# Two transformer blocks on one core: q and k as two-part fp32r rows in 32-row strips

## The chip, the cores and the metric

One core of a Trainium2 chip runs the whole program. The metric is the device time of one launch in microseconds, lower is better.

## The reference

Two conditioned transformer blocks run one after the other on x of shape (2, 512, 144): two sequences (b) of 512 tokens, width C = 144, 16 heads of 9. Both blocks have this form:

```
mod = silu(c) @ W_ada + b_ada                 # shift, scale, gate, twice
h = layernorm(x) * (1 + scale) + shift
q, k, v = h @ W_qkv + b_qkv
a = softmax(q k^T / 3) v                      # per head; block 1: causal mask
x = x + gate * (a @ W_proj + b_proj)
h = layernorm(x) * (1 + scale2) + shift2
x = x + gate2 * (act(h @ W_fc1 + b1) @ W_fc2 + b2)   # act: gelu in block 0, silu in block 1
```

The hidden width of the MLP is 576. Everything is float32. The program calls block 0 "layer 0" and block 1 "layer 1".

## The kernel before

Each of the five engines runs a list written at build time. `steps()` gives every piece of work (an item) a duration and what it has to follow; `plan()` puts the items of each engine in order and gives every TensorE item one of seven PSUM banks. There are streams: "max" (row maxima of the scores), "shift" (the maxima brought into the stacks), "attend" (scores and exps), "gather" (probs times V), and "side" (heads, tails, MLPs). The engines take their lists strictly in order, with semaphore waits inside.

Attention goes by groups of four heads, 16 groups in all: 8 in layer 0 and 8 in layer 1. For each group, TensorE first forms the scores with queries on partitions (L1129, 16 products of up to 512 keys), VectorE takes the negated row maximum of each (L1014), GpSimd splits the maxima in three bf16 parts (L768 to L771), TensorE transposes them (L1137), ScalarE copies them (L831) and a DMA of GpSimd puts them in rows of the q stack (L778). Then TensorE forms the scores once more with keys on partitions (L1147); with the extra rows they come out less their maximum, and ScalarE takes the exp (L841). The pv product (L1167) writes the four heads of a group in four column strips of one bank, with a column of ones for the sum. In layer 1 both score products have only the columns that the causal mask leaves (128, 256, 384 or 512), and a 128x128 matmul with the identity adds the mask to the diagonal block (L1131, L1150).

The scores have float32 accuracy through parts: q and k are each split in three bf16 parts, and six products of parts are stacked, 6 x 9 rows and three for the maximum, in tiles of 96 rows, QS and KS. To make them, the projection writes d-major rows, ScalarE and VectorE form the parts (L820, L995 to L998), SP writes them to DRAM (`qk_parts`, L638, L646) and reads them back into the stacks with repetition (L668). The stacks have to be zero first (L738 to L740, L823). In layer 1 the restack of a sequence follows its last layer-0 score product.

A wide projection (q/k and fc1, `wide_product`, L1064 to L1067) takes four fp32r matmuls: main channels high x high, high x low, low x high, and the 16 last channels with the bias in a stacked operand. VectorE forms the parts of the activations (L977 to L983) and ScalarE with GpSimd or VectorE those of the weights (`wsplit`). The gate products (L1095, L1096) and V (L1116) use plain fp32, which the trace shows as two records per matmul.

Of the kernel before, what the change touches and what calls it, by code (L numbers as in the profile page):

```python
# [7 lines left out]
U32 = mybir.dt.uint32  # L29
# [4 lines left out]
P = 128  # L34
# [9 lines left out]
QK = 2 * C  # L44
QKW = [128, 128, QK - 256]
# [4 lines left out]
SR = 96  # L50
EPS = 1e-6
# [7 lines left out]
Q_RUNS = [(0, 1, 3), (1, 1, 2), (2, 1, 1)]  # L59
K_RUNS = [(0, 3, 1), (0, 2, 1), (0, 1, 1)]  # L60
PRODUCTS = 6
MROW = PRODUCTS * D
KROWS = 96


# [13 lines left out]
def head_items(l, b):  # L79

    return ([("stats", l, b, 0, 0), ("norm", l, b, 0, 0), ("hT", l, b, 0, 1, 0), ("hT", l, b, 0, 0, 0)]
            + [("qk", l, b, c) for c in (2, 0, 1)] + [("v", l, b, i) for i in range(2)])


def mlp_items(l, b, s):

    items = []
    for c in range(NF + 2):
        if c < NF:
            items.append(("fc1", l, b, c, s))  # L90
        if c >= 1 and c - 1 < NF:
            items.append(("tanh", l, b, c - 1, s))
        if c >= 2:
            items.append(("gate", l, b, c - 2, s))
    return items


def tail_items(l, b):

    if part_with(l, b, 0) == 0:  # L100
        return ([("aT", l, b, r, 0) for r in range(2)] + [("proj", l, b, i) for i in range(2)]
                + [("stats", l, b, 1, 0), ("norm", l, b, 1, 0), ("hT", l, b, 1, 1, 0), ("hT", l, b, 1, 0, 0)]
                + mlp_items(l, b, 0) + [("fc2", l, b, i) for i in range(2)])
    items = [("aT", l, b, r, s) for s in (1, 2) for r in range(2)]
    items += [("proj", l, b, 0), ("stats", l, b, 1, 1), ("proj", l, b, 1), ("norm", l, b, 1, 1), ("stats", l, b, 1, 2),
              ("hT", l, b, 1, 1, 1), ("hT", l, b, 1, 0, 1), ("norm", l, b, 1, 2), ("hT", l, b, 1, 1, 2), ("hT", l, b, 1, 0, 2)]
# [3 lines left out]

SIDE = ([("stats", 0, 0, 0, 0), ("acol", 0, 0), ("norm", 0, 0, 0, 0), ("wsplit", 0, 0)] + head_items(0, 0)[2:4]
        + head_items(0, 1)[:1] + head_items(0, 0)[4:] + head_items(0, 1)[1:]
# [3 lines left out]
WEIGHTS = ([("acol", 0, 1), ("wsplit", 0, 1), ("wsplit", 1, 0), ("wsplit", 1, 1), ("acol", 1, 0), ("acol", 1, 1)]  # L116
           + [("agate", l, b) for l in range(L) for b in range(B)])
GROUPS = L * B * NG
BANKS = 7

# [11 lines left out]
def steps():  # L132

    out = []

    def add(stream, engine, item, ns, *after):
        out.append((stream, engine, item, ns, after))

    cost = {"acol": (950, 350), "agate": (980, 370), "v": (660, 370), "proj": (980, 370), "fc2": (2460, 370)}

    loaded = {("acol", 0, 0): 5500, ("wsplit", 0, 0): 7500, ("wsplit", 0, 1): 15500, ("stats", 0, 0, 0, 0): 4500,
              ("stats", 0, 1, 0, 0): 9500,
              ("acol", 0, 1): 36000, ("agate", 0, 0): 60000}
    norm = None
    for item in SIDE + WEIGHTS:
        kind, l, *rest = item
        b = rest[0]
        size = 0.5 if kind in ("stats", "norm", "hT", "aT", "fc1", "tanh", "gate") and rest[-1] else 1  # L150
        stream = "side" if item in SIDE else "weights"
        if kind in cost:
            after = {"acol": [], "agate": [],
                     "v": [("DVE", ("hT", l, b, 0, 0, 0))],
                     "proj": [*(("ACT", ("aT", l, b, r, part_with(l, b, rest[-1]))) for r in range(2)), ("POOL", ("agate", l, b))],
                     "fc2": [("DVE", ("gate", l, b, NF - 1, part_with(l, b, rest[-1])))]}[kind]
            add(stream, "PE", item, cost[kind][0], *after, loaded.get(item, 0))
            add(stream, "DVE", item, cost[kind][1], ("PE", item))
            if kind == "agate":
                add(stream, "POOL", item, 3200, ("DVE", item), 66000)  # L160
            if kind == "fc2" and l == L - 1:
                add("side", "SP", item, 500, ("DVE", item))
        elif kind == "wsplit":
            add(stream, "ACT", item, 1700, loaded.get(item, 0))
            if stream == "side":
                add(stream, "DVE", item, 1100, ("ACT", item))
            else:
                add(stream, "POOL", item, 6500 if b else 3500, ("ACT", item), 19000)
        elif kind == "stats":
# [4 lines left out]
            add("side", "POOL", item, 960, ("DVE", item), 0 if l or k or not b else 18500)  # L174
        elif kind == "norm":
            after = [("POOL", ("stats", *item[1:]))]
            if norm and norm != item[:4]:
                after += [("PE", ("hT", *norm[1:], r, 0)) for r in range(2)]
            norm = item[:4]
            add("side", "DVE", item, 1060 * size, *after)  # L180
        elif kind == "hT":
            k, r, _ = rest[1:]
            add("side", "PE", item, 430 * size, ("DVE", ("norm", l, b, k, rest[-1])))
            add("side", "ACT", item, (600 * size + 60), ("PE", item), ("DVE", ("acol", l, k)))

            add("side", "DVE", item, (1400 if r else 1070) * size + 2100 * (item[1:] == (0, 0, 0, 0, 0)), ("ACT", item))
        elif kind == "qk":
            add("side", "PE", item, 860, ("DVE", ("hT", l, b, 0, 0, 0)), ("POOL", ("wsplit", l, 0)) if l else ("DVE", ("wsplit", 0, 0)))
            c = rest[1]
            add("side", "ACT", item, 4000 if (l, b, c) == (0, 0, 1) else 480, ("PE", item))  # L190
            add("side", "DVE", item, 1700, ("ACT", item))
            after = [("PE", ("scores", (b + 1) * NG - 1, 15))] if l and c < 2 else []
# [1038 lines left out]
```

## Time and profile before

| | us |
|---|---|
| median of 3 runs | 380.48 |
| fastest, slowest | 379.99, 384.52 |
| span of the profiled execution, which is its time in the profile | 382.2 |

A row of the timeline has start, duration, engine, line, operation and the tiles, output first; x4 is a run of four. "96*128 96x512" is a weight tile of 96 rows and 128 columns and a moving tile of 96 rows and 512 columns. TensorE's ends are modelled and overlap, so distances between starts are what tells the pace. PE is TensorE, PEld its weight loads, DVE VectorE, ACT ScalarE, POOL GpSimd, SP SyncE. PEclk is the granted clock of TensorE, 1 at 2.4 GHz. fp32r tiles are named f32 in matmul rows.

### The profile page before, as it was taken

What the parts mean: (1) busy time and instruction counts of PE and PEld (TensorE: products, weight loads), DVE (VectorE), ACT (ScalarE), POOL (GpSimd) and SP (SyncE); (2) the same over time, 40 slices, a digit from 0 to 9 for tenths busy, and PEclk for the clock granted to TensorE, in tenths of its full rate; (3) what the DMA queues carried; (4) which work ended last, traced back from release to release, by engine and by line L of the source; (5) the groups of instructions that cost most, each with busy time, mean ns of one, the idle gap of its engine ahead of it and who ended that gap; (6) DMA issues with size and microseconds to landing.
All of it is one profiled execution on the core that took longest, in us unless ns stands there. A gap on an engine that the chain in (4) does not pass through costs nothing.

```text
span 382.2 us, 5927 instructions
## 1 busy us (share of the span) xinstructions
PE 305.8 (80%) x2020; PEld 165.7 (43%) x2020; DVE 260.8 (68%) x575; ACT 195.1 (51%) x414; POOL 72.8 (19%) x157
## 2 busy tenths in 40 slices
PE   2044399697999999889993879999953999999567
PEld 2023282122334363445341545565431565647366
DVE  6999589674858798996851667879633668831363
ACT  4037310274573755894781127745613456894352
POOL 5934500010102615501100010110100011010000
PEclk9999585588989999999997968999968799999969
DMA  6402645420000000000044100000451000000000
GB/s 173 116 0 79 143 92 157 103 72 17 1 2 2 0 4 1 2 1 3 1 121 100 60 7 0 3 1 13 128 96 53 3 1 3 3 1 17 16 2 31
DMA packets 11285, 15.57 MB, mean 41 GB/s; under 512 B 1774, under 2 KB 9909, under 8 KB 10824
## 3 DMA queue, kind: packets, MB, share of 16 engines
q1 hardware_dynamic: 10744, 15.00, 14.9%
q8 instruction: 16, 0.26, 0.3%
q0 software_dynamic: 512, 0.20, 0.2%
q14 instruction: 13, 0.11, 0.1%
HBM read 10.67 MB, written 4.13 MB: 39 GB/s over the span
## 4 chain that ended last, share of the span: by engine, by line
PE 53%; DVE 17%; DMA 14%; issue 6%; ACT 5%; SPq 4%; POOL 1%; DVEq 0%; ACTq 0%; POOLq 0%
PE PB L1147 11%; PE OB L1167 10%; DMA KS<-qk_parts 10%; PE PB L1129 9%; PE PB L1209 5%; DVE hn L968 4%; DMA QS<-mT 3%; SPq L668 3%; DVE negm L1014 3%; PE PB L1104 3%; DVE parts L998 2%; DVE rest L995 2%; PE PB L1174 2%; PE PB L1064 2%; PE PB L1150 1%
## 5 line engine op out<-in xcount | busy, mean ns | idle before, releaser
L1014 DVE TENSOR_REDUCE negm<-PB 128x1 f32<-128x512 f32 (+3 forms) x256 | 136.3, 583 | 62.4 <-PE PB L1131 39.2
L841 ACT ACTIVATE probs<-PB 128x512 f32<-128x512 f32 (+3 forms) x256 | 116.4, 521 | 80.2 <-PE PB L1150 47.0
L1129 PE MATMUL PB<-KS,QS 96*128 96x512 bf16 (+3 forms) x256 | 87.2, 387 | 21.1 <-DMA KS<-qk_parts 20.3
L1147 PE MATMUL PB<-QS,KS 96*128 96x512 bf16 (+3 forms) x256 | 81.4, 360 | 8.5 <-DMA QS<-mT 6.9
L1167 PE MATMUL OB<-probs,V 128*10 128x512 f32 (+3 forms) x512 | 59.7, 538 | 0.9 <-ACT probs L841 0.6
L1129 PEld LDWEIGHTS PB<-KS,QS 96*128 96x128 bf16 x256 | 26.2, 105 | 65.5 <-issue 42.0
L1147 PEld LDWEIGHTS PB<-QS,KS 96*128 96x128 bf16 x256 | 25.0, 101 | 52.9 <-issue 34.1
L768 POOL CAST msp<-negm 128x16 bf16<-128x16 f32 x16 | 4.3, 266 | 161.6 <-DVE negm L1014 161.6
L1104 PE MATMUL PB<-ident,hn 128*16 128x128 f32 (+1 forms) x64 | 12.1, 336 | 22.7 <-DVE hn L968 22.7
L1131 PE MATMUL PB<-mask_qk,identb 128*128 128x128 bf16 x128 | 29.4, 244 | 0.0
L1150 PE MATMUL PB<-mask_kq,identb 128*128 128x128 bf16 x128 | 27.0, 226 | 0.0
L831 ACT ACTIVATE mT<-PB 12x512 bf16<-12x512 bf16 x16 | 9.3, 581 | 27.2 <-PE PB L1137 27.1
L1036 DVE TENSOR_TENSOR X<-X,PB 128x288 f32<-128x288 f32 x16 | 7.3, 453 | 21.4 <-PE PB L1209 16.7
L1209 PE MATMUL PB<-g_fc,U 128*128 128x144 f32 (+1 forms) x160 | 20.7, 287 | 0.0
L735 POOL TENSOR_TENSOR rstd<-veps,half 128x4 f32<-128x4 f32 (+1 forms) x9 | 8.7, 969 | 61.8 <-DVE veps L958 61.7
L1209 PEld LDWEIGHTS PB<-g_fc,U 128*128 128x128 f32 (+1 forms) x160 | 20.0, 190 | 0.7 <-issue 0.4
L968 DVE TENSOR_SCALAR hn<-X,mean,rstd 128x144 f32<-128x144 f32 x32 | 19.5, 685 | 1.0 <-POOL rstd L735 1.0
L1053 DVE SCALAR_TENSOR_TENSOR U<-U,xh 128x512 f32<-128x512 f32 (+3 forms) x25 | 14.2, 578 | 8.0 <-ACT xh L877 7.5
L810 ACT ACTIVATE hT_r<-PB,mod_r 16x512 f32<-16x512 f32 (+1 forms) x9 | 6.5, 724 | 25.7 <-PE PB L1104 25.4
L1104 PEld LDWEIGHTS PB<-ident,hn 128*16 128x16 f32 (+1 forms) x64 | 7.7, 140 | 27.1 <-issue 13.4
L778 POOL DMA_DIRECT2D QS<-mT x16 | 9.6, 598 | 48.3 <-ACT mT L831 48.3
L850 ACT ACTIVATE OT<-OB 128x512 f32<-128x512 f32 x16 | 9.6, 599 | 16.2 <-PE OB L1167 16.2
(135 smaller groups left out, 453.6 us busy)
## 6 DMA issues: line engine op xcount, KB each, us to landing
qk_parts<-parts SPq DMA_DIRECT2D x8, 384.0 KB, 2.5
QS<-qk_parts SPq DMA_DIRECT2D x4, 324.0 KB
KS<-qk_parts SPq DMA_DIRECT2D x4, 324.0 KB
QS<-qk_parts SPq DMA_DIRECT2D x8, 108.0 KB
KS<-qk_parts SPq DMA_DIRECT2D x8, 108.0 KB
QS<-qk_parts SPq DMA_DIRECT2D x4, 216.0 KB
KS<-qk_parts SPq DMA_DIRECT2D x4, 216.0 KB
X<-in_x SPq DMA_DIRECT2D x2, 288.0 KB, 3.2
```

What stands on the lines that cost most here:

```text
L668: sp.dma_start(dst[row0:row0 + rows, h0:h1, :], src).then_inc(stacked[l * B + b][i], 16)
L841: nc.scalar.activation(probs[:, kt % 2, j, q0:T], bank_of(item)[:, q0:T], ACT.Exp, scale=SCALE).then_inc(bank_free[BANK[item]], 1)
L968: ins = nc.vector.tensor_scalar(hn[:, t, :], X[b][:, t, :], mean[:, t, 0:1], rstd[:, t:t + 1], ALU.subtract, ALU.mult)
L1014: nc.vector.tensor_reduce(negm[:, g % 2, qt, j:j + 1], bank[:, 0:keys_of(g // (B * NG), qt)], AX.X, ALU.max, negate=True).then_inc(bank_fr ...
L1053: nc.vector.scalar_tensor_tensor(u, u, 1.0, xh[0:w, c, tokens(s)], ALU.add, ALU.mult).then_inc(g_ready, 1)
L1104: ins = nc.tensor.transpose(bank[0:n, t * P:(t + 1) * P], src, ident[:, :])
L1129: ins = nc.tensor.matmul(o[:, 0:w], q, KS[b][0:KROWS, h + j, 0:w], start=True, stop=(l == 0))
L1131: ins = nc.tensor.matmul(o[:, w - P:w], identb[:, :], mask_qk[:, :], start=False, stop=True)
L1147: ins = nc.tensor.matmul(bank[:, q0:T], KS[b][0:KROWS, h + j, kt * P:(kt + 1) * P], QS[b][0:KROWS, h + j, q0:T], start=True, stop=(l == 0))
L1150: ins = nc.tensor.matmul(bank[:, q0:q0 + P], identb[:, :], mask_kq[:, :], start=False, stop=True)
L1167: ins = nc.tensor.matmul(OB[CT * j:CT * j + VW, q0:T], V[b][:, kt, h + j, :], probs[:, kt % 2, j, q0:T], start=(kt == 0), stop=(kt == NT - 1))
L1209: ins = nc.tensor.matmul(bank[:, t * C:(t + 1) * C], U[0:w, c, tok], g_fc2[l][b][0:w, c, :], start=(c == 0), stop=(c == NF - 1))
```

## The change

q and k now stay in SBUF. One head takes a strip of 32 partitions: 9 rows high, 9 rows high or low, 9 rows low or high, two rows for the maximum (high and low part) and three of zeros; four heads of a group fill 128 partitions. The projection's weights have the columns of a head three times, the low one negated, so one product writes all rows of a group; ScalarE rounds it to fp32r in the tile `QK`, and one VectorE pass subtracts, which leaves the low part where `low_row` is 1. The main channels are plain fp32, the last 16 channels with the bias one stacked fp32r operand. This stack is now made before the transpose ("hr" on VectorE, with modulation by rows). The maxima reach the q rows by matmul with an fp32r identity. The scores are products of 32 rows; the order of units goes through the heads first (`UNITS`). fc1 is also fp32 and one stack, layer 1's gate reads PSUM. The weights of layer 0 are spread by ScalarE, VectorE and GpSimd at the start, those of layer 1 by GpSimd ("stackw", "fcs"). The DMA through DRAM, the clearing of the stacks and the DMA of the maxima are gone. ScalarE's queue loads the first x and W_qkv. The durations in `steps()` were changed too.

```diff
-            + [("qk", l, b, c) for c in (2, 0, 1)] + [("v", l, b, i) for i in range(2)])
+            + [("qk", l, b, 0, w) for w in range(2)] + [("v", l, b, i) for i in range(2)]
+            + [("qk", l, b, g, w) for g in range(1, NG) for w in range(2)])
...
+UNITS = [(t, j) for t in range(NT) for j in range(HG)]
...
+        def strip(j):
+            return slice(CT * j, CT * j + CT)
+        def spread(w, which):
+            v = heads_in(w, which)
+            return (v[:, :, 0:3:2, :] if which else v[:, :, 0:2, :]), v[:, :, LOW[which]:LOW[which] + 1, :]
...
 (SP)
-                    sp.dma_start(scratch[l, b, c, :, 0:D - 1].rearrange("s d h t -> (d h) s t"),
-                                 parts[:, c, :, :]).then_inc(parts_out[c], 16)
...
-                                sp.dma_start(dst[row0:row0 + rows, h0:h1, :], src).then_inc(stacked[l * B + b][i], 16)
...
 (GpSimd)
-                        nc.gpsimd.memset(KS[0][0:KROWS, :, :].bitcast(U32), 0).then_inc(k_zeroed[0], 1)
...
+                    spread_heads(w_qk_s[0], w_s[0], 0).then_inc(wide_stack, 1)
+                    fill_late()
...
+                    link(nc.gpsimd.tensor_copy(s[:, :, :, MROW], m))
+                    nc.gpsimd.tensor_tensor(s[:, :, :, MROW + 1], m, s[:, :, :, MROW].bitcast(F32),
                                             ALU.subtract).then_inc(msplit_ready, 1)
-                    pool.dma_start(QS[b][MROW:MROW + 3, h:h + HG, :], mT[:, g % 2, :]).then_inc(m_in[g % 2], 16)
...
 (ScalarE)
+            act.dma_start(X[0][:, :, :], a["x"][0].rearrange("(t p) c -> p t c", p=P)).then_inc(x_in[0], 16)
...
+                    nc.scalar.activation(QK[b][:, g, w, :], bank_of(item), ACT.Copy).then_inc(high_ready, 1)
...
+                    nc.scalar.activation(QM[:, g % 2, :], bank_of(item), ACT.Copy).then_inc(bank_free[BANK[item]], 1)
...
 (VectorE)
+                    link(nc.vector.tensor_tensor(y, hn[:, t0:t1, P:C], row_of(SC), ALU.mult))
+                    link(nc.vector.tensor_tensor(y, y, row_of(SH), ALU.add))
...
+                    nc.vector.tensor_copy(hs[:, t0:t1, 65:65 + R], y)
+                    link(nc.vector.tensor_copy(hs[:, t0:t1, 1:1 + R], y))
+                    nc.vector.tensor_tensor(hs[:, t0:t1, 33:33 + R], y, hs[:, t0:t1, 1:1 + R].bitcast(F32),
+                                            ALU.subtract).then_inc(hr_ready, 1)
...
+                    s = QK[b][:, g, w, :]
+                    ins = nc.vector.scalar_tensor_tensor(s, bank, low_row[:, w:w + 1], s.bitcast(F32), ALU.mult, ALU.subtract)
...
 (TensorE)
+                    nc.tensor.matmul(bank, w_qk[l][:, w, cols], hT[:, :], start=True, stop=False)
+                    nc.tensor.matmul(bank, w_qk_s[l][:, w, cols], hT_s[:, :], start=False, stop=True).then_inc(filled_bank, 1)
...
-                    ins = nc.tensor.matmul(o[:, 0:w], q, KS[b][0:KROWS, h + j, 0:w], start=True, stop=(l == 0))
+                    rows = strip(j)
+                    ins = nc.tensor.matmul(bank[:, 0:w], QK[b][rows, g % NG, 0, qt * P:(qt + 1) * P],
+                                           QK[b][rows, g % NG, 1, 0:w], start=True, stop=(l == 0))
                     if l:
-                        ins = nc.tensor.matmul(o[:, w - P:w], identb[:, :], mask_qk[:, :], start=False, stop=True)
+                        ins = nc.tensor.matmul(bank[:, w - P:w], identb[:, :], mask_qk[:, :], start=False, stop=True)
...
+                    nc.tensor.matmul(bank, identr[:, :], QK[b][:, g % NG, 0, :], start=True, stop=False)
                     for t in range(NT):
-                        ins = nc.tensor.transpose(bank.bitcast(BF16)[0:3 * HG, t * P:(t + 1) * P],
-                                                  msp[:, t, :, :].rearrange("p s j -> p (s j)"), identb[:, :])
+                        ins = nc.tensor.matmul(bank[:, t * P:(t + 1) * P], msp[:, t, :], identr[:, :], start=False, stop=(t == NT - 1))
...
-                    ins = nc.tensor.matmul(bank[:, q0:T], KS[b][0:KROWS, h + j, kt * P:(kt + 1) * P],
-                                           QS[b][0:KROWS, h + j, q0:T], start=True, stop=(l == 0))
+                    ins = nc.tensor.matmul(bank[:, q0:T], QK[b][rows, g % NG, 1, kt * P:(kt + 1) * P],
+                                           QM[rows, g % 2, q0:T], start=True, stop=(l == 0))
                     if l:
                         ins = nc.tensor.matmul(bank[:, q0:q0 + P], identb[:, :], mask_kq[:, :], start=False, stop=True)
...
-                        ins = nc.tensor.matmul(o, aT_r[:, tok], g_proj_r[l][b][:, :], start=False, stop=True)
+                        ins = nc.tensor.matmul(o, aT_r[0:R + 1, tok], g_proj_r[l][b][:, :], start=False, stop=True)
...
+                    nc.tensor.matmul(bank[0:w, tok], w_fc1[l][:, cols], hT[:, tok], start=True, stop=False)
+                    nc.tensor.matmul(bank[0:w, tok], w_fc1_s[l][:, cols], hT_s[:, tok], start=False,
+                                     stop=True).then_inc(filled_bank, 1)
```

## Rows read from the trace of the kernel before

**Rows 1.** The page, part 1: busy time, share and instructions by engine.
```profile
PE 305.8 (80%) x2020; PEld 165.7 (43%) x2020; DVE 260.8 (68%) x575; ACT 195.1 (51%) x414; POOL 72.8 (19%) x157
```

**Rows 2.** The page, part 4: the chain that ended last, shares by line.
```profile
PE PB L1147 11%; PE OB L1167 10%; DMA KS<-qk_parts 10%; PE PB L1129 9%; PE PB L1209 5%; DVE hn L968 4%; DMA QS<-mT 3%; SPq L668 3%; DVE negm L1014 3%; PE PB L1104 3%; DVE parts L998 2%; DVE rest L995 2%; PE PB L1174 2%; PE PB L1064 2%; PE PB L1150 1%
```

**Rows 3.** Busy time of each engine in four stretches.
```profile
core 0: us, PE busy (x) PEld busy (x) DVE busy (x) ACT busy (x) POOL busy (x), PEclk, DMA share, GB/s
80.00:200.00 120.00, 114.87 (x673) 49.41 (x672) 90.88 (x179) 80.98 (x156) 25.60 (x61) 0.97 0.05 14
200.00:224.00 24.00, 14.10 (x97) 7.84 (x95) 10.27 (x32) 4.59 (x9) 0.82 (x4) 0.82 0.28 70
...
262.00:300.00 38.00, 26.37 (x203) 15.32 (x202) 20.68 (x48) 13.89 (x34) 2.22 (x9) 0.83 0.29 72
300.00:345.00 45.00, 45.00 (x423) 26.18 (x422) 30.36 (x78) 33.40 (x83) 6.23 (x17) 0.99 0.01 3
```

**Rows 4.** Timeline of the first 60 us: start, us, instruction.
```profile
10.14 11.44 DVE L968 TENSOR_SCALAR hn<-X,mean,rstd 128x144 f32<-128x144 f32 x4
...
13.04 3.50 POOL L739 MEMSET QS<- 96x4096 uint32 x1
...
37.34 1.14 DVE L968 TENSOR_SCALAR hn<-X,mean,rstd 128x144 f32<-128x144 f32 x4
...
55.24 16.82 DVE L1014 TENSOR_REDUCE negm<-PB 128x1 f32<-128x512 f32 x28
```

**Rows 5.** The chain that ended last, in order of time: start, us, piece.
```profile
67.75 5.31 DMA QS<-mT
...
202.79 18.68 DMA KS<-qk_parts
```

**Rows 6.** The page, part 5: layer scores; after the bars, idle time before them.
```profile
L1147 PE MATMUL PB<-QS,KS 96*128 96x512 bf16 (+3 forms) x256 | 81.4, 360 | 8.5 <-DMA QS<-mT 6.9
```

**Rows 7.** Timeline of TensorE, inside one wide product of fc1.
```profile
158.04 0.39 PE L1066 MATMUL PB<-hT_p,w_fc 128*128 128x512 f32 x1
158.28 0.40 PE L1067 MATMUL PB<-hT_s,w_fc_s 96*128 96x512 f32 x1
```

**Rows 8.** Timeline of TensorE, gate products between scores and a pv group.
```profile
117.43 0.51 PE L1096 MATMUL PB<-U,cond_wr 17*128 17x144 f32 x2
117.87 0.51 PE L1095 MATMUL PB<-xh,cond_w 128*128 128x144 f32 x2
118.31 0.51 PE L1096 MATMUL PB<-U,cond_wr 17*128 17x144 f32 x2
118.75 0.60 PE L1129 MATMUL PB<-KS,QS 96*128 96x512 bf16 x2
119.28 1.05 PE L1167 MATMUL OB<-probs,V 128*10 128x512 f32 x8
120.26 0.82 PE L1129 MATMUL PB<-KS,QS 96*128 96x512 bf16 x3
```

**Rows 9.** Timeline of TensorE, the transposes of mT and what follows.
```profile
116.11 0.39 PE L1137 MATMUL PB<-identb,msp 128*12 128x128 bf16 x4
116.43 0.39 PE L1129 MATMUL PB<-KS,QS 96*128 96x512 bf16 x1
```

**Rows 10.** Timeline of TensorE, inside the attention projection.
```profile
140.77 0.41 PE L1192 MATMUL PB<-g_proj,aT 128*128 128x144 f32 x2
141.02 0.41 PE L1193 MATMUL PB<-g_proj_r,aT_r 96*128 96x144 f32 x2
```

**Rows 11.** Timeline of TensorE, scores and masks of layer 1.
```profile
301.96 0.38 PE L1129 MATMUL PB<-KS,QS 96*128 96x512 bf16 x1
302.17 0.22 PE L1131 MATMUL PB<-mask_qk,identb 128*128 128x128 bf16 x1
302.23 0.33 PE L1147 MATMUL PB<-QS,KS 96*128 96x384 bf16 x1
```

**Rows 12.** Groups of instructions by line and shape: the masks of the maxima.
```profile
L1131 PE MATMUL PB<-mask_qk,identb 128*128 128x128 bf16 x128 | 29.4, 244 | 0.0
```

More of the change, by code:

```diff
@@ L50 @@
 SR = 96
+GW = NG * P
 EPS = 1e-6
@@ L129, in first_query, with freed_by @@
     return kt * P if l else 0
+def freed_by(item):
+    kind = item[0]
+    if kind in ("hT", "aT", "mT", "scores") or kind == "fc1" and item[1] == 0:
+        return "ACT", item
+    return "DVE", ("gate", *item[1:]) if kind == "fc1" else item
 def steps():
@@ L177, in steps @@
             if norm and norm != item[:4]:
-                after += [("PE", ("hT", *norm[1:], r, 0)) for r in range(2)]
-            norm = item[:4]
+                after += [("PE", ("hT", *norm[1:], 0, 0))]
             add("side", "DVE", item, 1060 * size, *after)
+        elif kind == "hr":
+            after = [("DVE", ("acol", l, rest[1]))]
+            if norm and norm != ("norm", *item[1:4]):
+                after += [("PE", ("hT", *norm[1:], 1, 0))]
+            norm = ("norm", *item[1:4])
+            add("side", "DVE", item, 900, *after)
@@ L187, in steps @@
         elif kind == "qk":
[L188 to L192, printed above, removed]
-            add("side", "SP", item, (500, 6700, 1000)[c], ("DVE", item), *after)
+            g = rest[1]
@@ L202, in steps @@
-            add("side", "ACT", item, 960 * size, ("PE", item), *mlp)
+            mlp = [("DVE", ("gate", *((l, 0) if b else (l - 1, 1)), c, 0))] if l or b else []
+            add("side", "PE", item, 1100 * size, *(("ACT", ("hT", l, b, 1, r, rest[-1])) for r in range(2)), ("POOL", ("fcs", l)))
+            add("side", "ACT", item, (430 * size + 90) * (1 if l else 2), ("PE", item), *mlp)
             if l == 0:
-                add("side", "DVE", item, 620 * size, ("ACT", item))
-        elif kind == "tanh" and l == 0:
-            add("side", "ACT", item, 520 * size, ("DVE", ("fc1", *item[1:])))
+                add("side", "DVE", item, 540 * size + 80, ("ACT", item))
+        elif kind == "tanh":
+            add("side", "ACT", item, 430 * size + 90, ("DVE", ("fc1", *item[1:])))
@@ L268, in plan @@
             if not isinstance(follow, int):
-                behind.setdefault(("POOL", follow[1]) if follow[0] == "rows" else follow, []).append((engine, item))
+                behind.setdefault(follow, []).append((engine, item))
         queue.append(item)
@@ L300, in plan @@
                 item = queues[q][at[q]]
[L301 to L309 removed]
+                start = max([free[engine], *(f if isinstance(f, int) else done.get(f, inf) + HANDOVER for f in after[engine, item])])
                 if start == inf:
@@ L347, in plan @@
             holder[k] = (item, stream)
-    return order, bank, before
-ORDER, BANK, BEFORE = plan()
+    return order, bank, before, max(done.values())
+ORDER, BANK, BEFORE, PLANNED = plan()
 def ordinals(kinds):
```

811 lines of the change are left out of this document (375 added, 436 removed).

## The prediction

> **What bounds the kernel now.** I read the page's totals first: TensorE is busy 80% of the span, VectorE 68% [rows 1]. The chain by line names the two score products, the probs-times-V product (pv) and, with 10%, the DMA that restacks q and k [rows 2]. Totals mix stages, so I read the stages next [rows 3]. Four kinds show. Before 55 us there is no attention: the first row maximum starts at 55.24 us [rows 4]. From 80 to 200 us TensorE is busy 114.9 of 120 us at clock 0.97 and from 300 to 345 us all of 45.0 at 0.99, while VectorE has 90.9 and 30.4: there TensorE sets the pace. From 200 to 224 and from 262 to 300 us it is busy 14.1 of 24 and 26.4 of 38 us, at clock 0.82 and 0.83, with the DMA engines at 0.28 to 0.29. These are the two layer-1 restacks, of which one piece alone, 18.7 us of the chain, is shown [rows 5]; the other is like it. "Busy" hides overlap of matmuls, so costs below are distances between starts.
>
> **What the change removes.** *Startup.* The normalisation of the first sequence takes 11.44 us beside GpSimd memsets of 3.50 us each that clear the q and k stacks; the same four instructions take 1.14 us later [rows 4]. After the change these memsets are gone, and so are the wide splits and the trip through DRAM. The new path to the first maximum: normalisation from 10.1 us 1.1 us, the five small tail-channel operations about 1.2, transposes and their copies about 3, the first two q/k products 2 x (5 x 512 columns)/1.2 GHz = 4.3, their two evictions 1.3: 21 us; with 3 us for GpSimd's spreading of the weight copies, which VectorE may again feel, 24. That is 31 earlier. TensorE work that was done before 55 us then lies in the attention phase: V and transposes of the second sequence and the rest of the projections, about 7. Net -24 (-30 to -15).
> *The restacks.* TensorE's idle time was 9.9 and 11.6 us in the two stretches, and the low clock took about 18% of the busy part, 2.5 and 4.5 us [rows 3]: 28. The 12 KB DMA with the row maxima takes 5.3 us on the chain for the first group [rows 5], much the same for the second; TensorE waited for such rows 6.9 us in all [rows 6], 7. Together -35 (-28 to -45, as the queues behind drain faster too). Issues on SP's queue cost nothing on either side: SP only stores and loads after this. GpSimd's 16 issues go as well; it is busy 19% [rows 1], and the new stacking on it is due at 22 us or later, in front of fc1 only.
> *The end.* Splits and layer 1's xh copy leave the last MLP: -2.
>
> **What it adds on TensorE.** *Projection and fc1.* A wide product is now 4 fp32r matmuls at 0.235 us from start to start [rows 7], 0.94. After it, one fp32 matmul of four passes, 4 x 512/2.4 GHz = 0.85, as the pv group shows (0.98 with its edges [rows 8]), and one of 0.235: 1.09. There are 32 for q/k in place of 12: 34.8 - 11.3 = +23.5. The 20 fc1 products gain 0.15 each, +3. The mT step becomes one 512-column fp32r matmul and four of 128 columns, 0.235 + 4 x 0.11 in place of 0.32 [rows 9], +0.36 x 16 = +6. Sum +32. VectorE loses about as much in splits as 32 subtractions of 0.6 us bring; it stays behind TensorE.
> *Strips.* Score matmuls now have 32 rows. The trace has no two row strips side by side. Above, four neighbours could overlap until their 128-column weight loads (0.107 us each, 128/1.2 GHz) are the limit; below they follow at 0.215 as the bf16 ones do [rows 11]. For 256 layer-0 matmuls that is -28 to 0. VectorE frees a bank only every 0.60 us (16.82 us for 28 [rows 4]), which breaks up the runs of four: I take -14.
> The Trainium skill (TensorE: Matmul & The Clock Gate, "Measured speedup vs the span model") gives 3.07 times for four row tiles of 512 columns; by it the 55 us of these matmuls would lose 37 and the sum below would be 23 lower, if VectorE let them come in fours. No row here shows it.
>
> *Changes of the array's shape.* This is the term that decides. The gate products take 128 rows and 17 rows (one 32-row strip) in turn [rows 8]. Each pair of 144-column records should take 0.245 us, as the 128- and 96-row pairs do, which follow at 0.25 [rows 10]. With the 17-row strip between, they follow at 0.44: 0.195 more at each change. The weight load can't run ahead, 0.1, and some 0.1 is the array emptying. The pv group, four column strips, confirms the 0.1: it starts 0.53 us after a pair of products of 0.215 each, and takes 0.98 for 0.853 of streaming [rows 8].
> In layer 1 each score product is followed by a mask matmul of 128 rows in the same bank. Now the two take w/2.4 + 0.06 us: 0.21 for 512 columns, 0.06 for the mask [rows 11]. After the change the first has 32 rows, the mask 128, so there are two changes of shape in every unit, and t-major order cannot group them. Price of a unit: +0.20 if only the emptying counts, +0.31 with the strip's fp32r weight load uncovered (the mask's bf16 load is small). There are 128 masks for the maxima [rows 12] and as many for the scores: +51 to +79, of which I take the middle, +65. A bound below is 0: if 32-row strips change nothing for the array, the whole term falls away. Nothing hides it where TensorE is full, as from 300 to 345 us; what waits behind a mask in TensorE's queue is the pv group, and ScalarE's exps and VectorE's maxima wait for the units.
> *Other edges.* Some 50 isolated full-array items of layer 0 (projections, transposes, fc1, fc2) now stand between strips, 0.2 each, and the projection's small operand shrinks from 96 to 17 rows, 32 more changes of 0.195; many items stand together, and pv had edges before. I take +12 (0 to +20).
>
> **Sum.** 382 - 24 - 35 - 2 + 32 - 14 + 12 + 65 = 416 us against the profiled execution's span of 382.2, which is 1.7 above the median of 380.48; so 414. The bounds of the terms give 388 to 438.
>
> **Rivals.**
> *No price for the shape (faster).* Strips of 32 rows and full-array matmuls follow without a gap: the 65 and 12 go and the time is 337, range 325 to 355. For it: the 0.195 is seen only with fp32 operands of 17 rows, never with fp32r and 32, and the removed startup and restacks, 59 us, are certain. Against it: the pv edges show the same 0.1 with another shape. The Trainium skill (TensorEngine Tiling (Array Packing), "Key Properties") says that changing the tiling mode drains TensorE; the trace agrees with 0.1 us per edge, and by this rule the rival fails. Chance 0.30.
> *Half hidden (same).* Only the emptying counts, partly under work that waits for banks anyway, so 25 to 40 for the masks in place of 65, 374 to 389. For it: PE waits on banks in the first and last groups. Chance 0.11.
> *A late start.* GpSimd's spreading and filling holds VectorE's normalisation as the memsets do now, 10 us [rows 4]: this adds 8 to 10 to whichever case holds, 424 with the forecast. Chance 0.04 on the forecast's side.
> *The forecast*, slower through the masks: 0.55. It decides from the point where the masks cost more than 382 - 351 = 31 us, that is 0.12 us a unit.
>
> **Numbers.** Within 2% (373 to 388) is about what a measurement of this kernel can't tell from no change. Faster by over 2%: the 0.30 and a third of the half-hidden case, 0.34. Within: the rest of it and the forecast's lower edge, 0.11. Slower: 0.55. The likeliest case alone has 388 to 438. For 8 in 10 the range must take in most of the first rival: 332 to 436 us leaves out some 0.11 below and 0.07 above.
>
> **What would show it.** In layer 1's rows, distance from a strip of w columns to its mask: w/2.4 + 0.1 if I am right, w/2.4 if the first rival is; the next strip then starts about 0.26 after the mask, else 0.06. TensorE would be full from the first layer-1 group to the last, near 20 us a group, not 11; VectorE's share falls below 60%. First maximum at 24 us; no idle stretch of TensorE above 3 us between the groups; a q/k product pair 1.09 apart; layer-0 strips at 0.11 to 0.22. The prediction is wrong if layer-1 units keep w/2.4 + 0.06, or if layer 0's groups are paced by VectorE's 16 x 0.60 us and TensorE has time to spare.

## The result, and the profile after

The changed kernel takes **556.0 us** (median of 4 runs, 554.2 to 559.1) against 380.6 for the kernel before (4 runs on the same chip, 380.0 to 384.5): 1.463 times as long (95% interval 1.453 to 1.472). The forecast was 414 us, so the direction was right and the size far off. The profiled run has a span of 552.4 us. Where the runs of one kernel lie more than 1.5% apart, times below are of the faster ones; the profiles of e1, e4 and e5 are of the slower of their two runs (mean clock 0.747, 0.664 and 0.753, the faster ones 0.782, 0.690 and 0.774).

The totals of the changed kernel, and TensorE's granted clock in 40 slices of the span (each digit in tenths of full speed; 5 is 1.2 GHz, 9 full), to be held against [rows 1]:

```profile
PE 525.5 (95%) x2091; PEld 266.6 (48%) x2091; DVE 241.6 (44%) x577; ACT 202.8 (37%) x402; POOL 48.9 (9%) x113
...
PEclk9955799755555999855555869975555555598959
```

TensorE has 71 more matmuls than before and 220 us more busy time; VectorE fell to 44%. The mean granted clock is 0.694, before it was 0.897. The chain of waits by line, which answers to [rows 2], has no DMA among its lines any more:

```profile
PE PB L1073 16%; PE PB L1050 15%; PE OB L1092 13%; PE PB L1029 6%; PE PB L1053 5%; PE PB L1126 5%; PE PB L1076 5%; PE PB L1138 4%; PE PB L1099 2%; PE PB L1014 2%; PE PB L1118 2%; PE PB L1117 2%; PE PB L1063 2%; ACT probs L741 2%; PE PB L1061 2%
```

L1050 and L1073 are the strips of the maxima and of the scores, L1053 and L1076 their masks, L1092 is pv. Stretches of the changed kernel, with the columns of [rows 3]:

```profile
65.00:100.00 35.00, 33.45 (x188) 14.75 (x180) 26.08 (x49) 24.48 (x46) 0.45 (x2) 1.00 0.01 1
105.00:175.00 70.00, 67.95 (x246) 36.61 (x245) 31.19 (x74) 23.33 (x42) 8.32 (x19) 0.50 0.00 1
180.00:225.00 45.00, 43.12 (x241) 20.79 (x240) 32.11 (x68) 29.02 (x55) 1.97 (x5) 1.00 0.00 1
235.00:305.00 70.00, 70.00 (x218) 33.42 (x215) 26.04 (x68) 14.70 (x27) 5.50 (x14) 0.50 0.00 0
370.00:480.00 110.00, 110.00 (x375) 52.58 (x374) 28.18 (x73) 30.42 (x67) 2.35 (x7) 0.50 0.00 1
```

Read the second number with the last but two: from 370 to 480 us TensorE is busy in all 110.00 us, and its clock is 0.50 throughout. This is not the low clock of [rows 3], which stood beside idle time and DMA. Here the engine is full and has half its speed. Adding up, over all matmul records, the distance to the next start, and sorting it by the clock at that start, 338 us of the changed kernel lie at 1.2 GHz and 205 at 2.4; of the kernel before, 70 and 302.

The moment of one such fall, in layer 1 (columns: start, us, instruction):

```profile
365.07 0.49 PE L1050 MATMUL PB<-QK 32*128 32x512 f32 x1
365.49 0.23 PE L1053 MATMUL PB<-mask_qk,identb 128*128 128x128 bf16 x1
365.65 0.38 PE L1073 MATMUL PB<-QM,QK 32*128 32x256 f32 x1
...
368.30 0.79 PE L1050 MATMUL PB<-QK 32*128 32x512 f32 x1
369.02 0.29 PE L1053 MATMUL PB<-mask_qk,identb 128*128 128x128 bf16 x1
369.24 0.58 PE L1073 MATMUL PB<-QM,QK 32*128 32x256 f32 x1
```

A unit of 512 columns with its mask takes 0.42 + 0.16 = 0.58 us at full clock (before: 0.21 + 0.06 = 0.27 [rows 11]) and 0.72 + 0.22 = 0.94 at half. There is no pause ahead of the fall.

The start, which answers to [rows 4], went as the prediction had it. VectorE:

```profile
13.16 1.14 DVE L875 TENSOR_SCALAR hn<-X,mean,rstd 128x144 f32<-128x144 f32 x4
...
25.79 1.88 DVE L922 TENSOR_REDUCE negm<-PB 128x1 f32<-128x512 f32 x3
```

### The profile page after: what moved, and what is told of

Same layout as the page of the kernel before. It is cut to its first block, busy times and chain, and to the rows that moved or that the text cites. A ratio compares the mean times of both kernels' runs of the same rounds, so it can differ in the third digit from the quotient of the medians.

```text
span 552.4 us, 6006 instructions
## 1 busy us (share of the span) xinstructions
PE 525.5 (95%) x2091; PEld 266.6 (48%) x2091; DVE 241.6 (44%) x577; ACT 202.8 (37%) x402; POOL 48.9 (9%) x113
## 4 chain that ended last, share of the span: by engine, by line
PE 91%; DVE 3%; ACT 2%; issue 2%; DMA 1%; SPq 0%; POOL 0%; POOLq 0%; ACTq 0%
PE PB L1073 16%; PE PB L1050 15%; PE OB L1092 13%; PE PB L1029 6%; PE PB L1053 5%; PE PB L1126 5%; PE PB L1076 5%; PE PB L1138 4%; PE PB L1099 2%; PE PB L1014 2%; PE PB L1118 2%; PE PB L1117 2%; PE PB L1063 2%; ACT probs L741 2%; PE PB L1061 2%
## 5 line engine op out<-in xcount | busy, mean ns | idle before, releaser
L1050 PE MATMUL PB<-QK 32*128 32x512 f32 (+3 forms) x256 | 124.0, 599 | 3.7 <-DVE negm L922 2.3
L1073 PE MATMUL PB<-QM,QK 32*128 32x512 f32 (+3 forms) x256 | 121.6, 572 | 2.6 <-ACT probs L741 2.1
L1050 PEld LDWEIGHTS PB<-QK 32*128 32x128 f32 x256 | 53.1, 247 | 62.9 <-issue 44.2
L1092 PE MATMUL OB<-probs,V 128*10 128x512 f32 (+3 forms) x512 | 79.2, 701 | 2.2 <-ACT probs L741 1.9
L1073 PEld LDWEIGHTS PB<-QM,QK 32*128 32x128 f32 x256 | 51.5, 236 | 55.5 <-issue 35.2
L1029 PE MATMUL PB<-hT,w_qk 128*128 128x512 f32 x64 | 40.1, 713 | 1.0 <-issue 0.7
L903 DVE SCALAR_TENSOR_TENSOR QK<-PB,low_row,QK 128x512 fp32r<-128x512 f32 x32 | 23.9, 746 | 25.4 <-ACT QK L726 25.4
L726 ACT ACTIVATE QK<-PB 128x512 fp32r<-128x512 f32 x32 | 19.1, 598 | 42.9 <-PE PB L1030 42.8
L1053 PE MATMUL PB<-mask_qk,identb 128*128 128x128 bf16 x128 | 34.8, 272 | 0.0
L1076 PE MATMUL PB<-mask_kq,identb 128*128 128x128 bf16 x128 | 33.7, 263 | 0.0
L1053 PEld LDWEIGHTS PB<-mask_qk,identb 128*128 128x128 bf16 x128 | 12.9, 101 | 33.5 <-issue 29.8
L1030 PE MATMUL PB<-hT_s,w_qk_s 96*128 96x512 f32 x32 | 28.9, 905 | 0.0
L1126 PE MATMUL PB<-hT,w_fc 128*128 128x512 f32 (+3 forms) x50 | 28.7, 665 | 0.0
L1076 PEld LDWEIGHTS PB<-mask_kq,identb 128*128 128x128 bf16 x128 | 12.8, 100 | 29.5 <-issue 24.5
```

Of the source, the lines that this page charges most:

```text
L903: ins = nc.vector.scalar_tensor_tensor(s, bank, low_row[:, w:w + 1], s.bitcast(F32), ALU.mult, ALU.subtract)
L1029: nc.tensor.matmul(bank, w_qk[l][:, w, cols], hT[:, :], start=True, stop=False)
L1030: nc.tensor.matmul(bank, w_qk_s[l][:, w, cols], hT_s[:, :], start=False, stop=True).then_inc(filled_bank, 1)
L1050: ins = nc.tensor.matmul(bank[:, 0:w], QK[b][rows, g % NG, 0, qt * P:(qt + 1) * P], QK[b][rows, g % NG, 1, 0:w], start=True, stop=(l == 0))
L1053: ins = nc.tensor.matmul(bank[:, w - P:w], identb[:, :], mask_qk[:, :], start=False, stop=True)
L1073: ins = nc.tensor.matmul(bank[:, q0:T], QK[b][rows, g % NG, 1, kt * P:(kt + 1) * P], QM[rows, g % 2, q0:T], start=True, stop=(l == 0))
```

## The experiments

The question was why TensorE has half its clock while it is full. **Theory A**: the emptying of the array at each change of shape (going from products of 32 rows to products of 128, or to the column strips of pv, and back) counts as a pause. **Theory B**: products of 32 rows bring the clock down while they fill TensorE. **Theory C**: the clock plays no part, only the shape's price. **Theory D**: the fp32 passes or the 17-row gate products do it.

**e1, no masks.** The changed kernel without its 256 masks, so without the changes of shape within units.

```
-                    if l:
-                        ins = nc.tensor.matmul(bank[:, w - P:w], identb[:, :], mask_qk[:, :], start=False, stop=True)
```
(and the same for the scores)

> The kernel after, with the 256 mask matmuls of layer 1 left out, so layer 1 is not causal here; the strips and everything else stay. The trace of the kernel after has TensorE busy 95% of 552 us, but at a mean granted clock of 0.694: 338 us at 1.2 GHz, 205 at 2.4. Theory A (the array empties at each change of shape, and a TensorE that stops so often is granted the low clock): the units of layer 1, now 175 us with their masks, fall to 36 to 50 us, the clock rises above 0.85, time 370 to 400 us. Rival B (thin products: 32 rows of 128 are too little work for the high clock, with or without masks): the clock stays at or below 0.72, layer 1's strips take 70 us or so, time 430 to 460 us. Rival C (the shape alone, the clock has nothing to do with either): 0.31 us x 256 and the mask streams go, 552 - 95 = 457 us or more at an unchanged clock in layer 0 and in layer 1.

Measured: 416.6 us (the other run 427.5), clock 0.782 (0.747). In 105 to 175 us, in layer 0, nothing changed; in layer 1 the clock came up only in part:

```profile
105.00:175.00 70.00, 67.95 (x259) 38.81 (x260) 31.53 (x79) 20.92 (x38) 5.59 (x14) 0.51 0.00 1
...
235.00:305.00 70.00, 67.00 (x327) 35.61 (x327) 39.85 (x110) 35.23 (x76) 6.90 (x17) 0.73 0.00 1
```

The time lies between A and B. But a clock of 0.73 in layer 1 with no mask left, and 0.51 in layer 0, which never had one, can't come from changes of shape within units. C fails, since the clock moved. There is something in A all the same: from the first maximum of layer 1 to its last exp the clock is 0.77 here and 0.64 in the changed kernel. Without masks the strips can also overlap, so this run alone doesn't say which of the two brought it up.

**e2, the whole array.** GpSimd copies each head's 32 rows of K into a tile of 128 rows that is otherwise zero, which adds nothing to the sums; every score product then has 128 rows.

```
+                        ins = nc.gpsimd.tensor_copy(KX[rows, g % 3, j, :], QK[b][rows, g % NG, 1, :].bitcast(F32))
-                    ins = nc.tensor.matmul(bank[:, 0:w], QK[b][rows, g % NG, 0, qt * P:(qt + 1) * P],
-                                           QK[b][rows, g % NG, 1, 0:w], start=True, stop=(l == 0))
+                    ins = nc.tensor.matmul(bank[:, 0:w], QK[b][:, g % NG, 0, qt * P:(qt + 1) * P],
+                                           KX[:, g % 3, j, 0:w], start=True, stop=(l == 0))
```

> The kernel after with one part undone: score products use all 128 rows. GpSimd copies each head's K strip into a tile that is zero in the other heads' rows (three groups are kept), so the products are the same numbers as in strips, from 128-row fp32r matmuls, and the masks have the same shape. The two raw small operands of fc1 and one of layer 1's q/k share the MLP's tile. No restacking DMA, projection in place as in the change. By the terms of the prediction: 416 less 65 (masks) less 12 (edges) plus 14 (no overlap of strips) plus 5 (fp32r at 0.235 for 0.215) = 358 us. Theory A and rival B both expect that, 345 to 375 us, with a clock above 0.88. If the fp32 projection or the early gate products lower the clock (rival D), the clock stays below 0.8 and the time is over 400 us.

Measured: **397.1 us** (396.3 to 397.3), 1.046 times the kernel before (1.038 to 1.053), clock 0.940. The same stretches as above:

```profile
PEclk9997899997568999999999999999999999999559
...
105.00:175.00 70.00, 69.22 (x346) 42.47 (x345) 47.67 (x112) 37.47 (x71) 16.56 (x30) 0.91 0.00 1
235.00:305.00 70.00, 68.47 (x468) 43.07 (x466) 42.66 (x100) 37.95 (x91) 12.04 (x23) 1.00 0.00 1
```

Going from 32 rows to 128, three quarters of them zeros, takes 159 us off. All else of the change (fp32 passes, 17-row operands) is still there, so D can't be the main cause. What stays above the expected 358 is read off TensorE's timeline:

```profile
303.52 0.48 PE L1105 MATMUL PB<-QM,KX 128*128 128x512 f32 x1
303.84 0.23 PE L1108 MATMUL PB<-mask_kq,identb 128*128 128x128 bf16 x1
303.88 0.48 PE L1082 MATMUL PB<-KX,QK 128*128 128x512 f32 x1
```

With no change of shape a unit takes 0.32 + 0.04 = 0.36 us where [rows 11] have 0.27: +0.086 for each of 256 units. In layer 0 neighbours follow at 0.235 instead of 0.215. Together that is 22 + 5 = 27 of the 39 us, which I put down to fp32r operands in place of bf16. No run changed the type alone, but the strips give the same step, 0.58 us a unit with fp32r and 0.48 with bf16 (e3 below). The weight loads suggest why; first the kernel before, then e2 (after the bars: busy us and mean ns of one), then one load of e2:

```profile
L1129 PEld LDWEIGHTS PB<-KS,QS 96*128 96x128 bf16 x256 | 26.2, 105 | 65.5 <-issue 42.0 <-DVE negm L1014 10.1 <-ACT probs L841 1.8
```
```profile
L1082 PEld LDWEIGHTS PB<-KX,QK 128*128 128x128 f32 x256 | 50.1, 199 | 24.2 <-issue 14.3 <-DVE negm L953 5.5 <-ACT probs L769 0.9
...
303.84 0.20 PEld L1082 LDWEIGHTS PB<-KX,QK 128*128 128x128 f32 x1
```

The load takes 199 ns instead of 105, and it starts with the mask, which streams for only 128/2.4 = 53 ns. The Trainium skill (TensorE: Matmul & The Clock Gate, "Weight-path perf modes — Fast Weight Load (FWL) and DoubleRow") keeps its faster weight load for types other than fp32. The trace agrees with that if fp32r counts as fp32, which the page doesn't say.

**e3, the kernel before with 32 rows.** Its bf16 stacks stay, but the score products read 32 of the 96 rows.

```
-                    q = QS[b][0:KROWS, h + j, qt * P:(qt + 1) * P]
-                    ins = nc.tensor.matmul(o[:, 0:w], q, KS[b][0:KROWS, h + j, 0:w], start=True, stop=(l == 0))
+                    q = QS[b][0:32, h + j, qt * P:(qt + 1) * P]
+                    ins = nc.tensor.matmul(o[:, 0:w], q, KS[b][0:32, h + j, 0:w], start=True, stop=(l == 0))
```

> The kernel before with its score products cut to the first 32 of their 96 rows (so not the full scores); masks, DMA and all else stay. This is the strip's shape alone, always the same strip, so nothing can overlap. Shape at a steady clock: 256 units x 0.2 to 0.25 (bf16 weights) = 51 to 64, and edges to other items 5 to 15: 435 to 460 us, clock 0.87 to 0.9. Theory A and rival B: the clock falls too, to 0.65 to 0.75, and the time passes 480 us. If the 0.31 us a unit of the kernel after came from fp32r and not from the shape: 380 to 395 us.

Measured: **534.1 us** (533.4 and 534.8), 1.407 times the kernel before (1.394 to 1.421), clock 0.638. With startup, restacks, projection and bf16 left as they were, the fewer rows alone bring some 154 us. First the kernel before, then this run:

```profile
105.00:175.00 70.00, 67.66 (x394) 32.15 (x393) 55.24 (x108) 46.01 (x88) 21.14 (x49) 0.98 0.01 2
...
105.00:175.00 70.00, 70.00 (x227) 21.90 (x223) 29.75 (x52) 24.01 (x43) 9.67 (x25) 0.50 0.00 1
```

This stretch is in layer 0, where neither kernel has masks. Changes of shape don't tell the two apart: between neighbouring records of TensorE I count 55 of them in the row of before, mostly into and out of pv, and 50 in that of e3. The clock is 0.98 in the one and 0.50 in the other. Both levels can be seen within 1.3 us of layer 1:

```profile
327.11 0.38 PE L1147 MATMUL PB<-QS,KS 32*128 32x512 bf16 x1
327.43 0.23 PE L1150 MATMUL PB<-mask_kq,identb 128*128 128x128 bf16 x1
327.59 0.57 PE L1147 MATMUL PB<-QS,KS 32*128 32x512 bf16 x1
328.09 0.29 PE L1150 MATMUL PB<-mask_kq,identb 128*128 128x128 bf16 x1
328.31 0.60 PE L1147 MATMUL PB<-QS,KS 32*128 32x512 bf16 x1
```

At full clock 0.32 + 0.16 = 0.48: two edges of 0.10 more than [rows 11].

**e4, masks of 32 rows too.** As e3, with the masks cut to 32 rows (`identb[0:32, :], mask_qk[0:32, :]`), so no unit changes the shape.

> As the run before, but the mask matmuls also use only 32 rows (identity and mask cut to 32 rows, so the mask is incomplete): units of layer 1 have no change of shape within, only at pv and side items. Theory A: the clock is back near 0.88 and the time is 385 to 405 us, the rest being edges of side items. Rival B (thin products): the clock stays at 0.65 to 0.75 and the time is over 440 us. Rival C: as A, since the clock never fell.

Measured: 472.0 us (the other run 489.8), clock 0.690 (0.664). Layer 0 has no masks and so repeats e3. First a full stretch of layer 1, then units of layer 1 at full clock:

```profile
380.00:430.00 50.00, 50.00 (x272) 24.91 (x270) 22.76 (x58) 21.14 (x48) 3.86 (x11) 0.50 0.01 1
```
```profile
302.29 0.27 PE L1129 MATMUL PB<-KS,QS 32*128 32x256 bf16 x1
302.40 0.21 PE L1131 MATMUL PB<-mask_qk,identb 32*128 32x128 bf16 x1
302.45 0.32 PE L1129 MATMUL PB<-KS,QS 32*128 32x384 bf16 x1
```

The units are back at w/2.4 + 0.06 (0.16 for 256 columns). The price of the shape is gone, and e4 is 62 us faster than e3 (256 units x 2 edges x 0.10 = 51 at full clock), but the clock is low all the same: 0.50 with TensorE busy in 50.00 of 50 us. So A fails as the main cause, and B holds. The edges do add to the low clock: over layer 1 it is 0.64 here and 0.59 in e3, though the masks now have fewer rows. How much they add in the changed kernel was not separated.

**e5 and e6, strips in one layer only.** e2 with the changed kernel's strips in layer 1 (e5) or in layer 0 (e6; there the condition is `l == 1`).

```
+                    if l == 0:
+                        ins = nc.tensor.matmul(bank[:, 0:w], QK[b][:, g % NG, 0, qt * P:(qt + 1) * P],
+                                               KX[:, g % 3, j, 0:w], start=True, stop=(l == 0))
+                    else:
+                        ins = nc.tensor.matmul(bank[:, 0:w], QK[b][rows, g % NG, 0, qt * P:(qt + 1) * P],
+                                               QK[b][rows, g % NG, 1, 0:w], start=True, stop=(l == 0))
```

> The changed kernel with the score products of layer 0 over the whole array (as in e2), those of layer 1 in 32-row strips. Between the first product and the first mask of layer 1 the changed kernel takes 25 us more than e2 (235.5 against 210.4 us), after it 132 us more (325 against 193). Theory B (products of 32 rows lower the granted clock while they fill TensorE): layer 0 as in e2 with a clock of 0.9 or more up to 210 us, layer 1 at 0.5 to 0.7; 397 + 132 = 529 us, 510 to 545. Theory A (changes of shape and the emptying of the array lower it): the same layer 1, so the same time; this run tells A from B only together with e6. If something that is the same in both layers lowers the clock (the fp32 passes of the projection, theory D), layer 0 shows it too, below 0.8, and the time is above 550.

> The changed kernel with 32-row strips in layer 0 alone and the score products of layer 1, with their masks, over the whole array. No unit changes the array's shape; strips of layer 0 overlap. Theory B: the granted clock falls in layer 0 wherever the strips come in runs, 0.5 to 0.75 there, and returns to 0.9 or more in layer 1; 397 + 25 = 422 us, 410 to 440. Theory A: with some 100 changes of shape in place of 600 the clock stays at 0.9 or more in both layers, the strips overlap, and the time is 380 to 397. Theory C (no clock effect of strips): as A.

Measured: e5 523.3 us (the other run 534.6); e6 420.8 us (418.7 and 422.8), 1.101 times the kernel before (1.088 to 1.114). First e5, then e6:

```profile
PEclk9989999679999999755776568555555555588859
...
105.00:175.00 70.00, 69.22 (x351) 42.34 (x350) 49.10 (x112) 39.47 (x75) 16.58 (x30) 0.94 0.00 1
235.00:305.00 70.00, 69.84 (x242) 37.82 (x241) 30.16 (x83) 23.47 (x46) 5.33 (x10) 0.62 0.00 1
```
```profile
PEclk9995559986555555599999999999999999999959
...
105.00:175.00 70.00, 68.51 (x247) 37.49 (x246) 30.91 (x77) 22.13 (x40) 9.60 (x21) 0.50 0.00 1
235.00:305.00 70.00, 67.84 (x406) 43.19 (x409) 47.80 (x123) 31.59 (x63) 15.00 (x32) 1.00 0.00 1
```

The clock follows the strips from layer to layer, and the times nearly add up: 397 + 24 (layer 0) + 126 (layer 1) = 547, against 556. (Held against the kernel before of its own session, the 24 is 21.) In e6 the strips overlap and there are no masks between them; the clock is 0.50 there, and 24 us are lost where the prediction had a gain of 14.

**e7, 64 rows.** As e3 with `[0:64, ...]`.

> The kernel before with its score products cut from 96 to 64 rows (32 rows gave 534 us at a clock of 0.64; 96 rows 380 at 0.90); the masks keep 128 rows. What is left out: the last 32 rows of each stack. Theory B, graded (the clock follows the share of rows that a product uses): between, a clock of 0.72 to 0.85 and 440 to 500 us. Theory B, only for the thinnest products: the clock is 0.88 or more, and only the 256 units' changes of shape are paid, 380 + 51 to 79 = 430 to 460. If 64 rows are treated as 96 are in every respect: 375 to 390 us.

Measured: 451.2 us (447.9 and 454.6), 1.181 times the kernel before (1.160 to 1.202), clock 0.796. Two stretches of layer 0, and three rows of layer 1:

```profile
105.00:135.00 30.00, 30.00 (x93) 9.34 (x93) 12.68 (x25) 9.98 (x18) 2.66 (x8) 0.50 0.00 1
150.00:200.00 50.00, 48.75 (x279) 22.67 (x277) 42.45 (x91) 32.73 (x63) 13.38 (x27) 1.00 0.01 2
```
```profile
418.09 0.33 PE L1147 MATMUL PB<-QS,KS 64*128 64x384 bf16 x1
418.35 0.23 PE L1150 MATMUL PB<-mask_kq,identb 128*128 128x128 bf16 x1
418.51 0.28 PE L1147 MATMUL PB<-QS,KS 64*128 64x256 bf16 x1
```

The effect is graded: over the whole run 96 rows give a clock of 0.90, 64 give 0.80, 32 give 0.64, with 70, 181 and 380 us of TensorE's time at 1.2 GHz. The edges between 64 and 128 rows cost the same 0.10 each (0.26 for 384 columns, then 0.16).

**e8 to e12: the certain part, and a faster kernel.** Four drop masks or move them; e11 isolates the restacks.

> e2 (the changed kernel with full-array score products) without the 128 masks in the maxima of layer 1: the shift is then the maximum over whole key tiles, which is at least that of the allowed keys and cancels in the softmax. In e2 a score product of 512 columns is followed by its mask after 0.321 us and the next product comes 0.039 after that, 0.360 a unit; without a mask two such products are 0.235 apart. So 128 x 0.125 = 16 us less: 381 us (376 to 388), if TensorE stays the bound and the clock stays at 0.94. If masks of 128 columns had hidden weight loads of the fp32r products, less is gained: 388 to 395.

```
-                        ins = nc.tensor.matmul(bank[:, w - P:w], identb[:, :], mask_qk[:, :], start=False, stop=True)
```

Measured: 385.8 us (6 runs, 381.5 to 387.2), 1.010 times the kernel before (1.004 to 1.016), and 11 us less than e2 where 16 were expected (14 when each is held against the kernel before of its own session).

> e8 with the score masks of layer 1 taken off TensorE too: one GpSimd affine_select per key tile sets the forbidden part of the 4 heads' probabilities (128 x 4 x 128) to 0 before the probs-times-V product. e8 gained 11 us for 128 masks. If TensorE stays the bound and GpSimd's select (estimate 1 to 2 us, from its 0.63 us for 32x512) hides behind the next tile's exponentials: 386 - 11 = 375 us, 368 to 380, faster than both kernels by little. If the product waits for GpSimd (32 selects in a queue that also copies K): no gain or a loss, 384 to 400.

```
+                    nc.gpsimd.affine_select(out=d, in_=d, compare_op=ALU.is_ge, fill=0.0, base=0,
+                                            pattern=[[0, HG], [1, P]], channel_multiplier=-1).then_inc(masked, 1)
```

Measured: **374.4 us** (373.3 to 378.5), 0.983 times the kernel before (0.976 to 0.989): the fastest of the kernels here that leave out nothing of the function, though by less than 2%. The select costs GpSimd 0.63 us for 128x512, and pv waits for it 1.2 us in all:

```profile
L707 POOL TENSOR_SCALAR_AFFINE_SELECT probs<-probs 128x512 f32<-128x512 f32 x32 | 20.2, 634 | 47.0 <-ACT probs L779 46.7
...
L1132 PE MATMUL OB<-probs,V 128*10 128x512 f32 (+3 forms) x512 | 57.2, 522 | 1.4 <-POOL probs L707 1.2 <-ACT probs L779 0.3
```

> The kernel before without the 128 masks in the maxima of layer 1 (the shift is the maximum over whole key tiles). A mask there costs 0.06 us from start to start and TensorE is full in layer 1: 380 - 128 x 0.06 = 372 us, 370 to 377. If VectorE or the restacks set the pace there, no change: 378 to 383.

Measured: 377.4 us (376.5 to 378.5), 0.989 times the kernel before (0.984 to 0.993): 3 us instead of 8.

> e10 with the score masks on GpSimd as in e9. If both sets of 128 masks are worth 0.06 us each on TensorE and the selects are hidden: 380 - 15 = 365 us, 360 to 371, the fastest of all kernels here. If the probs-times-V products wait for GpSimd: 372 to 390, slower than e10.

Measured: 377.4 us (8 runs, 376.2 to 379.5), 0.992 times (0.988 to 0.997), no better than e10; 365 was expected. Freeing TensorE in the kernel before mainly lengthens its waits: busy time from 300 to 345 us fell from 45.00 [rows 3] to 42.24, while the restacks in front stayed as they were. The changed kernel's structure, once its strips are gone, can use what the masks free; the other hardly can.

> The kernel before without the DMAs that carry the bf16 parts to DRAM and back into the stacks, and without the waits for them; the stacks keep the zeros and ones of their memsets, so the scores are not those of the inputs. Splits, projections, memsets and all products stay. What it isolates is the part of the prediction that was certain: the waits at the start and in front of layer 1. The prediction gives 28 us for the two layer-1 restacks and, of the startup, what lies after the splits, 55.2 - 40 = 15 us: 380 - 43 = 337 us, 325 to 350, clock above 0.9. If the restacks were mostly hidden behind other groups: 360 to 375. If the clock falls because TensorE then runs without pauses (theory E, a limit on sustained work): a clock below 0.85 in the full stretches and 350 or more.

```
-                                sp.dma_start(dst[row0:row0 + rows, h0:h1, :], src).then_inc(stacked[l * B + b][i], 16)
```
(with the DMAs to DRAM and the waits for them; the stacks hold only the zeros and ones of their memsets)

Measured: 345.4 us (345.35 and 345.43), 0.905 times the kernel before (0.899 to 0.910), clock 0.94.

```profile
80.00:200.00 120.00, 116.90 (x723) 52.46 (x721) 95.17 (x194) 81.98 (x157) 25.01 (x61) 1.00 0.01 2
...
240.00:300.00 60.00, 59.24 (x560) 35.21 (x559) 47.89 (x122) 40.13 (x98) 7.87 (x25) 1.00 0.01 3
```

TensorE has 59.24 of 60 us at clock 1.00 with 96-row products: steady work by itself doesn't lower the clock (the theory E of this run). Its operands are mostly zeros, so it doesn't say whether the data matter. 43 us were expected. The first maximum stayed at 55.4 us, with the splits and memsets still in front of it, so the 15 us of the startup didn't come; the 35 us come from behind it, the restacks and the clock around them.

## Why the prediction was wrong

**What it got right.** *The direction*: slower through the masks. By the estimate below the changed kernel would take 552 - 127 = 425 us even at full clock, so the sign wasn't luck. *Startup*: the normalisation takes 1.14 us and the first maximum comes at 25.8 us against 24 forecast. *The restacks*: 28 us without the row-maxima DMA; e11, which keeps that DMA, gained 35. *The projection*: q/k pairs were to be 1.09 apart. They are 1.10 at full clock:

```profile
71.67 0.79 PE L1030 MATMUL PB<-hT_s,w_qk_s 96*128 96x512 f32 x1
...
72.77 0.79 PE L1030 MATMUL PB<-hT_s,w_qk_s 96*128 96x512 f32 x1
...
96.79 0.51 PE L1073 MATMUL PB<-QM,QK 32*128 32x512 f32 x2
```

*Strips overlap*: the last row has two of 512 columns ended within 0.51 us. *The price of the shape*: +0.20 to +0.31 us a unit were the bounds; at full clock it is 0.58 - 0.27 = +0.31, the upper one. In its parts: the unit of e2 costs +0.09 (fp32r loads), the change of shape +0.22. The mask comes 0.42 after its strip and the next strip 0.16 after the mask, where I had 0.31 and 0.26; the sum, 0.57 forecast and 0.58 measured, was right. The rival without a price for the shape falls with it: e3 and e4 differ by 62 us.

**What failed: the clock that every term took for granted.** All costs of the sum are distances at 2.4 GHz, and the low clock of the kernel before entered only as something that goes away with the restacks. No step asked what strips would do to it. At half clock the 512-column unit takes 0.94 / 0.58 = 1.6 times as long. With that ratio as an estimate for everything, the changed kernel's 338 us at 1.2 GHz would be 211, so 127 us are lost to the clock; in the kernel before 70 us would be 44, so 26 are, of which the sum gave back 7. The clock thus costs 108 us more than the sum had. The masks at their upper bound cost 79 instead of 65, another 14. That makes 122 of the 552 - 416 = 136 us between sum and profiled span. The step to e2 checks the estimate: there the time at 1.2 GHz goes from 338 to 48 us, 290 x (1 - 1/1.6) = 109, and the change of shape 0.22 x 256 = 56; together 165, and 159 were measured. The last 14 of the 136 are not assigned; e2 too is 12 us above what its fp32r operands explain.

The range had a fault of its own. Its terms, each at its bound and simply added, give 360 to 468 us; the stated 388 to 438 is what comes out when their distances are combined as the root of the sum of squares, which the prediction doesn't say. 556 lies outside both, because no term and no rival held a fall of the clock.

**Whether the profile of before could have told.** In part. Its stretches show a clock near 1 where 96-row products fill TensorE [rows 3], so I took a full TensorE for a fast one. What it couldn't show is a full TensorE on 32-row products. The Trainium skill (TensorE: Matmul & The Clock Gate, "Why this matters for your kernels") puts a fall in mid-kernel down to idle gaps of TensorE and recommends row groups for products of few rows. Here the measurement decides otherwise: 110.00 of 110 us busy at clock 0.50, and the strips that start together cost 24 us in layer 0.

**What stays open.** How the chip weighs activity was not measured. Strips did run at full clock in the changed kernel, from 65 to 100, from 180 to 225 and from 332 to 362 us. In each of these stretches 8 fp32 q/k products of 512 columns over 128 rows (16 records of L1029) and 8 over 96 rows stood between them. The last of the three is in layer 1, with masks:

```profile
332.00:362.00 30.00, 30.00 (x151) 15.84 (x149) 14.29 (x41) 15.69 (x32) 1.41 (x3) 1.00 0.00 1
```

It has 61 changes of shape in 30 us at clock 1.00; from 105 to 175 us there are 68 in 70 us at 0.50. That is one more sign against theory A. The clock was also low from 28 to 62 us, from the first strips on. The fall at 103 us came after a run of mod and gate products of 2 to 16 columns, every other one of 17 rows, and the strips that followed kept it low until 178 us:

```profile
102.78 0.40 PE L991 MATMUL PB<-w_ada,cond_w 128*128 128x16 f32 x2
103.11 0.35 PE L992 MATMUL PB<-w_ada_r,cond_wr 17*128 17x16 f32 x1
103.11 0.76 PE L1050 MATMUL PB<-QK 32*128 32x512 f32 x1
```

e2 falls within the same products, at 93 us, and is back at 121 us, up to the last MLP at 366 us (the 5s in its row of the clock); its score products have 128 rows there, not 32. So the mix of thin and full products seems to decide, not the strip alone; no run varied the mix by itself.

## What to carry to other kernels

A product of few rows takes as long as one of 96 or 128 (e4's units take w/2.4 + 0.06 us, as those of [rows 11] do), and when such products fill TensorE they can cost it half its clock; before cutting rows, or packing heads in strips, price every row of the sum at both clocks. Zero rows that fill up the array are cheap: one copy of K by GpSimd was worth 159 us here. And a change that frees an engine pays only where that engine is the bound: moving the masks gave e9 11 us and e12 nothing.

## What the runs showed of the hardware

- With TensorE full or nearly so (67.6 to 70.0 of 70 us, from 105 to 175 us), the kernels with 96-row or 128-row score products had a granted clock of 0.91 to 1.00, those with 32-row ones 0.50 or 0.51; 64-row products came in stretches of either. The type (bf16 in e3, fp32r in the changed kernel) and the overlap of strips (e6) made no difference there, nor did the 96 rows of zeros in e2's K.
- Edges between shapes lower the clock further: over layer 1 it was 0.59 with them (e3) and 0.64 without (e4).
- Each edge between 32 or 64 rows and 128 costs 0.10 us at full clock (e3: 0.32 + 0.16 for a unit that takes 0.21 + 0.06). A unit whose strip is fp32r takes 0.10 more (0.42 + 0.16).
- A weight load of 128 fp32r columns takes 199 ns, one of bf16 105. With fp32r operands a unit of product and mask takes 0.09 us more (0.36 against 0.27); that the longer load isn't covered behind the mask is the likely reason, not a tested one.
- The same mask product is worth 0.09 us in e2 (11 us for 128) and 0.02 us in the kernel before (3 us for 128), where waits stand beside it.
- An affine_select over 128x512 takes GpSimd 0.63 us, and pv waited for 32 of them 1.2 us in all.
